# A four-layer graph network: nodes' last rows in three parts instead of two, and the norm of a part between the merges

## What is computed

```python
def _layernorm(x, axis=-1, eps=1e-05):
    m = jnp.mean(x, axis=axis, keepdims=True)
    v = jnp.var(x, axis=axis, keepdims=True)
    return (x - m) / jnp.sqrt(v + eps)
...
    edge_index = jnp.stack([src, dst])        # 3125 nodes, 53125 edges sorted by dst, 64 channels
    h = jnp.maximum(_layernorm(x, axis=-1), 0.0)
    x = x + _L0_gnn_ref(h, edge_weight, ...)  # mean over a node's edges of h[src] * weight, times W_neigh; plus h times W_self
    h = jnp.maximum(_layernorm(x, axis=-1), 0.0)
    x = x + _L1_gnn_ref(src, dst, h, edge_attr_3, ...)
    # d = two small layers on edge_attr_3; logits = (h@W1)[dst] - (h@W2)[src] + d
    # softmax over a node's edges, weighted sum of (h@W3)[src] + d
    h = jnp.maximum(_layernorm(x, axis=-1), 0.0)
    x = x + _L2_gnn_ref(h, edge_attr_64, ...)
    # edge layer on [h[src], edge_attr_64] with batch norm and silu; mean per node; node layer with batch norm and silu
    h = jnp.maximum(_layernorm(x, axis=-1), 0.0)
    x = x + _L3_gnn_ref(h, edge_index)        # sum of h[src] over a node's edges
    return x
```

## Time and profile before

| | us |
|---|---|
| median of 3 runs | 2112.9 |
| lowest, highest | 2112.38, 2113.97 |
| the profiled execution, device time | 2112.08 |
| its span in the trace | 2110.3 |

### The profile page before, as it was taken

One profiled execution on the slowest core, in us unless ns is written; L12 is line 12 of the kernel. 1 busy time (PEld: TensorE's weight loads), 2 busy tenths in 40 slices (PEclk: granted clock), 3 DMA queues, 4 the chain that ended last, 5 costly groups with the idle time before them and its releaser, 6 DMA issues. The chain is left out here.

```text
span 2110.3 us, 23002 instructions
## 1 busy us (share of the span) xinstructions
PE 1472.3 (70%) x6831; PEld 1142.4 (54%) x6831; DVE 1570.8 (74%) x2458; ACT 900.5 (43%) x1176; POOL 1348.8 (64%) x1404
## 2 busy tenths in 40 slices
PE   2777777877644666666662299999967428999990
PEld 1555655645543554555551177777745226877770
DVE  6877677767655898898995767777768367999882
ACT  1333333333226666776751144444437213434340
POOL 5777777777627777767773377777700417777754
PEclk9776676666666887787775599999975558999995
DMA  5422222222223554555552244444435313434331
GB/s 127 108 80 75 84 74 82 81 76 81 76 59 108 156 175 154 178 175 179 174 167 89 68 89 93 91 95 96 93 90 182 95 25 75 111 93 106 92 91 37
DMA packets 216424, 220.57 MB, mean 105 GB/s; under 512 B 107182, under 2 KB 170115, under 8 KB 216067
## 3 DMA queue, kind: packets, MB, share of 16 engines
q1 hardware_dynamic: 167555, 147.32, 23.6%
q0 software_dynamic: 45024, 58.36, 12.9%
q10 hardware_dynamic: 3744, 13.63, 1.7%
HBM read 117.72 MB, written 101.46 MB: 104 GB/s over the span
## 5 line engine op out<-in xcount | busy, mean ns | idle before, releaser
L605 POOL DMA_INDIRECT gathered<-table,idx x1272 | 1232.8, 969 | 528.7 <-issue 391.5
L1670 DVE COPY_PREDICATED spare<-spare,psum 64x512 f32<-64x512 uint8 x294 | 216.6, 737 | 145.8 <-ACT spare L1290 106.1
L941 PE MATMUL psum<-rounded 128*128 128x512 f32 x1092 | 266.2, 401 | 23.8 <-DVE rounded L1772 23.8
L941 PEld LDWEIGHTS psum<-rounded 128*128 128x128 f32 x1092 | 206.9, 193 | 66.7 <-issue 24.1
L638 POOL DMA_INDIRECT arena<-scan,rowidx x100 | 102.3, 1023 | 190.4 <-DMA scan<-ea 124.2
L1290 ACT ACTIVATE spare<-psum 64x512 f32<-64x512 f32 x82 | 48.3, 589 | 315.6 <-PE psum L941 315.0
L1092 ACT ACTIVATE arena<-psum 128x1024 f32<-128x1024 f32 x52 | 53.2, 1024 | 235.6 <-PE psum L728 143.7
L742 PE MATMUL psum<-ident,arena 128*128 128x128 f32 x416 | 99.5, 385 | 41.6 <-DVE arena L1522 20.8
L1772 DVE TENSOR_SCALAR_CACHE_REDUCE rounded<-spare,rowcol 128x1024 fp32r<-128x1024 uint16 x105 | 128.3, 1265 | 0.0
L941 PE MATMUL psum<-rounded_keep 128*128 128x512 f32 x480 | 127.4, 414 | 0.0
L1531 DVE TENSOR_TENSOR arena<-gathered,wgt 128x512 f32<-128x512 f32 x52 | 36.2, 696 | 116.6 <-DMA gathered<-table,idx 116.5
(11 more groups left out here) (270 smaller groups left out, 3449.7 us busy)
## 6 DMA issues: line engine op xcount, KB each, us to landing
scan<-arena SPq DMA_DIRECT2D x52, 768.0 KB, 4.0
scan<-ostage SPq DMA_DIRECT2D x130, 256.0 KB, 2.2
gathered<-table,idx POOLq DMA_INDIRECT x1272
d_mlp<-arena ACTq DMA_DIRECT2D x26, 512.0 KB, 2.7
arena<-d_mlp SPq DMA_DIRECT2D x52, 256.0 KB, 4.4
ea<-in_edge_attr SPq DMA_DIRECT2D x104, 128.0 KB
spare<-src_row SPq DMA_DIRECT2D x98, 128.0 KB, 3.4
spare<-src_quarter SPq DMA_DIRECT2D x98, 96.0 KB, 3.1
```

What stands on the lines that cost most here:

```text
L605: pool.indirect_dma_start(out=out[:, j, hf, :], out_offset=None, in_=tab[layer], in_offset=bass.IndirectOffsetOnAxis(ap=idx[:, j, hf * NCH ...
L941: last = nc.tensor.matmul(P[:, bank + t, :], parts[layer][n][:, b:b + 2, :].rearrange("p b d -> p (b d)"), tile(layer, m, u)[:, hf * CH:(h ...
L1670: picked = v.copy_predicated(rows[m % 2][halves[hf], :], quarter[m % 2][halves[hf], q - 1, :], P[halves[q % 2], bank + q // 2, :])
```

## The change

`PARTS` becomes a with blocks 0 to 7, b with 8 to 15, c with 16 to 24, and `PAIRS` 4, 4 and 5 pairs. Everything that runs for each part now runs three times: the merges of all four layers, layer 1's and layer 2's norms, transposes, products, copies and table stores, and the output stores (four with the last, incomplete block). Layer 3's norm and its table keep the two parts of before (`LAST_PARTS`). GpSimd and ScalarE wait for 48 instead of 32 of the table's semaphore in layers 1 and 2.

In layer 0 the orders of VectorE, TensorE and ScalarE change: the norm of a comes behind the merge of b and ahead of the merge of c, and the tables of a ahead of the neighbour product of c. In layer 3 the spread tail is added to x once for all blocks ahead of the parts, and each part's rows are then added to x directly. The lists of stages, which number the semaphore's counts in the order of the work, follow.

```diff
-PARTS = {"a": slice(0, 16), "b": slice(16, NB)}
-PAIRS = {"a": range(0, 8), "b": range(8, NPAIR)}
+PARTS = {"a": slice(0, 8), "b": slice(8, 16), "c": slice(16, NB)}
+PAIRS = {"a": range(0, 4), "b": range(4, 8), "c": range(8, NPAIR)}
+LAST_PARTS = {"a": slice(0, 16), "b": slice(16, NB)}
+LAST_PAIRS = {"a": range(0, 8), "b": range(8, NPAIR)}
...
             def node_table(layer, made, src):
-                for part, r in PARTS.items():
+                for part, r in (LAST_PARTS if layer == 3 else PARTS).items():
...
-            sp.wait_ge(*stage("w1 copied b"))
+            sp.wait_ge(*stage("w1 copied c"))
...
+            for part, r in PARTS.items():
+                whole = min(r.stop, NB - 1)
+                sp.wait_ge(*stage(f"x4 made {part}"))
+                sp.dma_start(out[r.start * 128:whole * 128, :].rearrange("(b p) d -> p b d", p=128),
+                             x[:, r.start:whole, :]).then_inc(S("out stored"), 16)
             sp.dma_start(out[(NB - 1) * 128:N, :], x[0:NLAST, NB - 1, :]).then_inc(S("out stored"), 16)
-            sp.wait_ge(S("out stored"), 48)
+            sp.wait_ge(S("out stored"), 64)
...
-            pool.wait_ge(S("table stored", 1), 32)
+            pool.wait_ge(S("table stored", 1), 48)
             wide_gathers()
             last_rows(1, 3 * D)
-            pool.wait_ge(S("table stored", 2), 32)
+            pool.wait_ge(S("table stored", 2), 48)
...
+            def l0_neighbours(part):
                 to_channels(tmp, f"L0 merged {part}", f"agg0 transposed {part}", part)
                 pe.wait_ge(*stage(f"agg0T copied {part}"))
                 pe.wait_ge(*stage("x self added"))
                 linear(W[:, WNEIGH_T, :], 4, f"neigh made {part}", part)
-            for part in PARTS:
+
+            def l1_tables(part):
                 to_channels(h, f"h1 made {part}", f"h1 transposed {part}", part)
                 pe.wait_ge(*stage(f"h1T copied {part}"))
                 linear(W[:, W2, :], 4, f"w2 made {part}", part)
                 linear(W[:, W3, :], 0, f"w3 made {part}", part)
+
+            l0_neighbours("a")
+            l0_neighbours("b")
+            l1_tables("a")
+            l0_neighbours("c")
+            l1_tables("b")
+            l1_tables("c")
...
-            for part, banks in (("a", (0, 1)), ("b", (2, 3))):
+            for part, banks in (("a", (0,)), ("b", (1,)), ("c", (2, 3))):
                 to_channels(tmp, f"L2 merged {part}", f"agg2 transposed {part}", part)
...
+            copy_channels(hT, "agg0 transposed", "agg0T copied", "a")
+            copy_channels(hT, "agg0 transposed", "agg0T copied", "b")
+            l1_tables("a")
+            copy_channels(hT, "agg0 transposed", "agg0T copied", "c")
+            l1_tables("b")
+            l1_tables("c")
...
-            def merge_sum(layer, factor, done=None, then=None):
+            def spans_merged(layer, factor):
...
+            def last_rows_merged(layer, factor, part, into, done):
+                r = PARTS[part]
+                dve.wait_ge(S(f"last rows {part}"), n_last_rows(layer, part))
+                step(v.tensor_tensor(aggs[:, r, :], aggs[:, r, :], bc(factor, r), ALU.mult))
+                step(v.tensor_tensor(into[:, r, :], into[:, r, :], aggs[:, r, :], ALU.add))
+                dve.sem_inc(stage_of(f"{done} {part}"), 1)
+
+            def h1_made(part):
                 dve.wait_ge(*stage(f"neigh made {part}"))
-                add_to_x(4, r)
-                layernorm_relu(h, f"h1 made {part}", r)
+                add_to_x(4, PARTS[part])
+                layernorm_relu(h, f"h1 made {part}", PARTS[part])
+
+            spans_merged(0, invdeg[:, :])
+            last_rows_merged(0, invdeg[:, :], "a", tmp, "L0 merged")
+            last_rows_merged(0, invdeg[:, :], "b", tmp, "L0 merged")
+            h1_made("a")
+            last_rows_merged(0, invdeg[:, :], "c", tmp, "L0 merged")
+            h1_made("b")
+            h1_made("c")
...
-            merge_sum(2, invdeg[:, :], "L2 merged")
+            spans_merged(2, invdeg[:, :])
+            for part in PARTS:
+                last_rows_merged(2, invdeg[:, :], part, tmp, "L2 merged")
...
-            for part, r in PARTS.items():
+            for part, r in LAST_PARTS.items():
                 dve.wait_ge(*stage(f"z transposed {part}"))
...
-            def finish(part, r):
-                step(v.tensor_tensor(x[:, r, :], x[:, r, :], tmp[:, r, :], ALU.add))
-                dve.sem_inc(stage_of(f"x4 made {part}"), 1)
-
-            merge_sum(3, degpos[:, :], then=finish)
+            spans_merged(3, degpos[:, :])
+            step(v.tensor_tensor(x[:, 0:NB, :], x[:, 0:NB, :], tmp[:, 0:NB, :], ALU.add))
+            for part in PARTS:
+                last_rows_merged(3, degpos[:, :], part, x, "x4 made")
```

More of the change, by code:

```diff
@@ L163, in build @@
                 "index parts made", "counts copied", "rowidx made", "span parts made", "rows indexed", "x self added", "L0 merged a", "L0 merged b",
-                "h1 made a", "h1 made b", "h1 split", "merge diffs made", "L1 tail merged", "h2 made a",
-                "h2 made b", "w1a split", "edge bn mean part made", "edge bn var part made", "edge bn ready",
-                "L2 merged a", "L2 merged b", "node bn mean part made", "node bn var part made",
-                "node bn ready", "h3 made a", "h3 made b", "h3 split", "x4 made a", "x4 made b"),
+                "h1 made a", "L0 merged c", "h1 made b", "h1 made c", "h1 split", "merge diffs made", "L1 tail merged", "h2 made a",
+                "h2 made b", "h2 made c", "w1a split", "edge bn mean part made", "edge bn var part made", "edge bn ready",
+                "L2 merged a", "L2 merged b", "L2 merged c", "node bn mean part made", "node bn var part made",
+                "node bn ready", "h3 made a", "h3 made b", "h3 split", "x4 made a", "x4 made b", "x4 made c"),
         }
@@ L518, in _ @@
             l1_store(NIT - 1, 1)
-            sp.wait_ge(*stage("L0 merged b"))
+            sp.wait_ge(*stage("L0 merged c"))
             tail_row(1, 3 * D)
@@ L925, in _ @@
                 linear(W[:, W1A, :], 4, f"w1a made {part}", part)
[L926 removed]
+            pe.wait_ge(*stage("w1a copied c"))
             def multiply(layer, m, hf, bank):
@@ L1020, in _ @@
             combine("node bn")
-            for part in PARTS:
+            for part in LAST_PARTS:
                 pe.wait_ge(*stage(f"z activated {part}"))
-                for q in PAIRS[part]:
+                for q in LAST_PAIRS[part]:
                     last = nc.tensor.transpose(PF[:, q * 128:(q + 1) * 128], agg[:, q * 128:(q + 1) * 128],
@@ L1149, in copy_nodes, with l1_tables @@
                      f"{need} {part}", f"{done} {part}", scale=scale)
-            for part in PARTS:
-                copy_channels(hT, "agg0 transposed", "agg0T copied", part)
-            for part in PARTS:
+            def l1_tables(part):
                 copy_channels(hT, "h1 transposed", "h1T copied", part)
@@ L1233, in _ @@
                 l1_onehot(0, u)
-            act.wait_ge(S("table stored", 1), 32)
+            act.wait_ge(S("table stored", 1), 48)
             act.wait_ge(S("w1 stored"), 16)
@@ L1357, in _ @@
             act.wait_ge(*stage("node bn ready"))
-            for part in PARTS:
-                c = slice(PAIRS[part].start * 128, PAIRS[part].stop * 128)
+            for part in LAST_PARTS:
+                c = slice(LAST_PAIRS[part].start * 128, LAST_PAIRS[part].stop * 128)
                 nc.scalar.activation(agg[:, c], tabs[:, 0:NPAIR, :].rearrange("p b d -> p (b d)")[:, c],
@@ L1635, in merge_sum @@
                 step(v.memset(tmp[:, NB:NBP, :], 0.0))
-                for part, r in PARTS.items():
-                    dve.wait_ge(S(f"last rows {part}"), n_last_rows(layer, part))
-                    step(v.tensor_tensor(aggs[:, r, :], aggs[:, r, :], bc(factor, r), ALU.mult))
-                    step(v.tensor_tensor(tmp[:, r, :], tmp[:, r, :], aggs[:, r, :], ALU.add))
-                    if done:
-                        dve.sem_inc(stage_of(f"{done} {part}"), 1)
-                    else:
-                        then(part, r)
-            merge_sum(0, invdeg[:, :], "L0 merged")
-            for part, r in PARTS.items():
-                dve.wait_ge(*stage(f"neigh made {part}"))
-                add_to_x(4, r)
-                layernorm_relu(h, f"h1 made {part}", r)
+            def last_rows_merged(layer, factor, part, into, done):
[5 more added lines that the diff above has]
+            def h1_made(part):
+                dve.wait_ge(*stage(f"neigh made {part}"))
+                add_to_x(4, PARTS[part])
[7 more added lines that the diff above has]
+            h1_made("c")
             def split_table(layer, table, done):
```

20 lines of the change are left out of this document (7 added, 13 removed), and 13 rows, old and new, of the table stages.

## The result

| | before | changed |
|---|---|---|
| median, us | 2112.38 | 2105.32 |
| lowest, highest, us | 2109.33, 2114.09 | 2100.33, 2107.45 |
| runs | 7 | 7 |
| profiled execution: device time, span | 2112.08, 2110.3 | 2106.72, 2105.0 |

The changed kernel is 7.1 us faster, ratio 0.9965 with a 95% interval of 0.9953 to 0.9978. The forecast was 2103.5 with 2098.5 to 2108.5: the time lies 1.8 us above the forecast, inside the range.

A forecast was written before the change was run, and what follows sets the result against it. No single owner: each edge loop has its own bound, with short serial pieces between, which the change targets. Gains 3.0 + 5.6 + 0 + 0.8 = 9.4 us from 2112.9 gave 2103.5 us, range 2098.5 to 2108.5.

The forecast's parts named there:

- Layer 0: 3.0 expected: Layer 0's piece: norm of a fills VectorE's wait between merges, 3.3 us less 0.3 for held gathers; between 0 and 5.0.
- the 0.3 I took: Layer 0: part c's rows come 0.3 us later because new VectorE operations run beside GpSimd's row issues; possible 0 to 3.4.
- I had left that at 4.6: Layer 0's end: from the last copy's end to layer 1's first gather, taken as 4.6 us, as before.
- the clock would stay slow: Layer 0, part c's tables: TensorE stays slow, 20 matmuls taking 4.2 us at 0.21 each; 3.3 us gained, not 5.0.
- the cover of 1.7 us: Layer 0: TensorE has c's neighbour product ready at 606.5, 1.7 us before VectorE asks for it at 608.2.
- Layer 1: 5.6 expected: Layer 1's merge and norm on VectorE: 10.0 us earlier start less 4.4 for a third part, 5.6 us gained.
- Layers 2 and 3: 0 and 0.8 expected: Layer 2: last part unchanged, 0 us; layer 3: tail add moves into VectorE's idle time, 0.8 us gained.
- (1): Rival, layer 0: TensorE's fast clock holds through part c's tables, 1.7 us more gained, 2101.8 us; chance 0.13.
- (2): Rival: new operations hold GpSimd, layer 0 gains 0 and layer 1 loses 0.5; 5.9 us gained, 2107.0; chance 0.11.
- (3): Rival: layer 1's edge loop falls into another pace, up to 3.3 us per further late chunk; 2120.0 us; chance 0.09.
- called itself wrong if the loops differed by over 3 us: Sign of error: the loops between the pieces differ by over 3 us from before.
- (4): Rival: layer 1's parts b and c are not covered, only layers 0 and 3 gain, 3.8 us, 2109.1; chance 0.05.

The follow-up runs named there:

- the other trace: The changed kernel itself, unaltered, traced once more in a later run: 2105.11 us, ratio 0.9965 to the kernel before.
- e7: Changed kernel plus eight unread TensorE transposes behind c's neighbour product and eight behind b's tables in layer 0: 2103.66 us, ratio 0.9962 to before.
- e3: Kernel before with three parts in layers 2 and 3 alone and layer 3's early add of the tail share: ratio 0.9984 to before.
- e12: Changed kernel plus layer 0's idle transposes, two parts in layer 2, small operands in PSUM in every layer: 2102.51 us, ratio 0.9938 to before.
- e9: Changed kernel plus idle transposes, two parts in layer 2, layer 3's old merge with 22 and 3 blocks: 2689.70 us (slower chip), ratio 0.9982 to before.

## Why the prediction was right

**Layer 0: 3.0 expected, 3.0 and 3.5 measured.** VectorE's side came as worked out. Of the 3.3 us the longer row issues took 0.9 (34.30 less 33.36), three times the 0.3 I took; the last norm is 2.3 us earlier, close to 3.3 less 0.9. The new operations cost 0.8 of it, in both traces: 0.4 beside b's merge and a's norm, the place that the sum had in view, and 0.4 at a's own merge (586.18), beside issue 16, which the sum left out. The rest is where the older 1600-wide operations happened to fall; in the other trace they cost 0.3 less than before. Two misses made the 3.0 even, which is luck: this one, and the way from the last norm's end to the first gather, 11.19 us where it was 11.90, most of it between the last copy's end and the gather (4.09, before 4.63). I had left that at 4.6. It is 4.1 in all traces with three parts in layer 0 and 4.6 to 4.9 in those with two, so the change does it; by what way isn't shown. That the clock would stay slow was right, and so was the cover of 1.7 us ahead of c's product.

**Layer 1: 5.6 expected, 5.3 and 5.1 measured.** The first part starts 15.81 us behind the span-row issue, 15.8 by the sum's own starts. The parts take 12.1, 12.1 and 12.8 us, where I had 11.8 for the first two; from its start to the end of the last norm they take 36.99 (1151.32 to 1188.31), not 36.7. The new collisions, 1.5 us more of row issues, lie under the cover, as said, but they used it up in part: the rows land 1.2 us ahead of b's start and 0.8 ahead of c's, where I had 1.9 and 2.0.

**Layers 2 and 3: 0 and 0.8 expected, -0.6 and 0.5 measured, in the other trace -0.4 and -0.6.** This is the part that was mis-sized. The prediction priced the held issues in layer 0 only, took them as covered in layer 1, and for layers 2 and 3 wrote 0 and "moves into VectorE's idle time". VectorE was idle there, but GpSimd wasn't: its 25 issues are the path, and each issue that is held moves all behind it. The terms were 0.6 and 0.1 in layer 2 (rows 33.08 and 32.65 against 32.51) and 0.3 and 1.4 in layer 3. More traces show that these terms are chance: before's own merges are held in some traces too. In the mean over all of them layer 2 lost nothing, so its 0 stands, and layer 3 lost some 0.2 where 0.8 was to be gained. That add of 0.8 is the term that failed.

**The rivals.** (1), the fast clock, has the right price (1.7 for the matmuls in e7, 2.0 for the piece), but didn't come by itself. (2), GpSimd held to the full, was too dear in size but right in kind, and it lacked its main place, layer 3. (3), a loop in another pace: ScalarE's waits behind gathers are what they were the earlier trace rows, and the loops scatter by 3 us in sum also where nothing was changed in them. The prediction called itself wrong if the loops differed by over 3 us, and in the profiled pair they differ by 2.9 (1834.1 against 1831.1); the equal means say that this is scatter. It didn't come; that it can't come isn't shown.
```profile
ACT arena L1210 <- DMA gathered<-table,idx: 48.7, 15, 5.2
```
(4), layer 1 uncovered, fell with the rows of its three parts: b and c start 0.14 us behind the part ahead of them.

What stays open: how much of the 1.2 us between the pieces' 8.3 and the median's 7.1 is the loops' scatter and how much is the change's doing. The few traces can't tell.

## What to carry to other kernels

An idle engine is a place for work only if the work takes nothing from the engine that is not idle there. Before moving an operation into a wait, ask which engine's instructions end that wait, and whether the operation reads what they read: here GpSimd's row issues ended it, an add with two SBUF operands could hold each for as long as it ran, and the same add with one operand in PSUM held none. Cut a serial piece into so many parts that the two engines reach the last part together, and no further: with three parts layer 1 was there, and parts of 6, 8 and 11 blocks instead of 8, 8 and 9 cost 1.5 us.

## What the runs showed of the hardware

- A row issue of 0.94 us that meets a VectorE operation with two SBUF operands already under way ends 0.81 or 0.82 us behind that operation's end, in all 58 cases of four traces and in all 204 of the fourteen; the longest of the 58 took 2.55 us. Which of the two comes first decides: 0.05 us ahead or more the operation held the issue, 0.04 us ahead or later it did not. VectorE was never held by over 0.08 us.
- The same kernel takes 2112 to 2116 us on some chips and 2693 or 2726 on others, nearly all of it in the edge loops (31 to 33% longer). The pieces keep their length: layer 1's with three parts within 0.3 us, layer 0's within 1.0, layer 2's within 1.6, which its held issues explain. Only layer 0's piece with the transposes differs more (61.2 and 64.3 us, at a fast and a slow clock).
- In three of the seven traces from the slower chips VectorE stood for 16.9 to 19.3 us ahead of one add, for a cause that the profile only calls remote. Layer 0's piece in e3, VectorE:
```profile
846.57 1.82 DVE L1456 TENSOR_TENSOR x<-x,psum 128x1600 f32<-128x1600 f32 x1 [19.32 <-remote]
```
- With eight transposes ahead of a gap TensorE ran at 2.4 GHz behind a gap of 1.65 us (e7, 46 matmuls in 5.40 us) and not behind gaps of 2.63 and 3.15 us (e12 and e9, 7.90 and 7.88). That the length of the gap decides isn't shown, since the clock had also risen at different times: in e7 it is still at 0.50 from 609 to 612 and at 1.00 from 615 to 618, in e12 already at 1.00 from 607 to 616 and at 0.50 from 619 to 622.
